# ScalarE writes v's rounded part from PSUM and VectorE takes v's remainder there, in a two-layer attention and coupling kernel

## The reference

```
x = x + attention(layernorm(x))
x = x + coupling_network(layernorm(x))
```

```
k = apply_rope(x @ Wk.T)
v = x @ Wv.T
q = apply_rope(einsum('btd,hkd->bhtk', x, Wq))
w = softmax(where(causal, q k^T * HS**-0.5, -inf))
out = (w v, heads side by side) @ Wo.T
```

## The kernel before, in words

| bank of | is next taken by | VectorE's steps just ahead of its `project` step |
|---|---|---|
| project (group 0, tile 0) | project (group 0, tile 2) | turn_p (1, 1), norm of group 1, scores (2, 3) |
| project (group 0, tile 3) | turn_p (2, 2) | scores (3, 0), scale of group 1, close 1 |
| project (group 1, tile 0) | turn_p (3, 2) | norm of the next batch's group 0, close 2 |
| project (group 1, tile 1) | turn_p (3, 3) | turn_p (3, 1), turn_p (3, 2) |

## Time and profile before

### The profile page before, as it was taken

The page is one execution under the profiler, slowest core; times in us unless marked ns, Lnnn a source line. Parts: engine busy times, 40 slices in busy tenths (PEclk is TensorE's granted clock), DMA queues, the critical chain, the costliest instruction groups (busy, mean ns, idle before and its releaser), DMA issues. The chain is left out here.

```text
span 926.4 us, 15342 instructions
## 1 busy us (share of the span) xinstructions
PE 814.3 (88%) x4368; PEld 644.3 (70%) x4368; DVE 720.2 (78%) x1567; ACT 464.4 (50%) x1020; POOL 363.7 (39%) x377
## 2 busy tenths in 40 slices
PE   4689999998999989999999789988879889999952
PEld 3578788887888868888888557666656666666731
DVE  6779898896998978989978736777777878776575
ACT  2355565554565645565555255444444445444421
POOL 4535644364256434642460014333333334333331
PEclk9889999999999999999999899877897989877865
DMA  6000011101110110011000250000000100000011
GB/s 186 1 1 29 19 46 47 46 1 50 46 36 12 47 49 24 24 47 46 2 0 2 81 192 1 23 24 23 19 28 0 41 27 24 24 24 23 11 35 45
DMA packets 34588, 32.60 MB, mean 35 GB/s; under 512 B 3524, under 2 KB 34244, under 8 KB 34500
## 3 DMA queue, kind: packets, MB, share of 16 engines
q1 hardware_dynamic: 34500, 31.56, 10.7%
HBM read 16.88 MB, written 14.68 MB: 34 GB/s over the span
## 5 line engine op out<-in xcount | busy, mean ns | idle before, releaser
L507 ACT ACTIVATE pT_hi<-bank 128x512 fp32r<-128x512 f32 x192 | 90.9, 492 | 104.6 <-PE bank L843 96.1
L554 ACT ACTIVATE x_all<-scores_ps,neg_max 128x384 f32<-128x384 f32 (+7 forms) x128 | 94.6, 739 | 46.3 <-DVE neg_max L684 42.4
L580 DVE TENSOR_TENSOR pT_lo<-bank,pT_hi 128x512 fp32r<-128x512 f32 x192 | 100.7, 547 | 21.3 <-ACT pT_hi L507 21.3
L684 DVE TENSOR_REDUCE neg_max<-scores_ps 128x1 f32<-128x384 f32 (+7 forms) x128 | 95.3, 749 | 23.9 <-PE scores_ps L816 17.9
L843 PE MATMUL bank<-ident,x_all 128*128 128x128 f32 x576 | 92.7, 279 | 22.3 <-DVE pT_lo L580 17.3
L384 POOL TENSOR_TENSOR rope_a<-x_all,cos_sb 128x384 f32<-128x384 f32 x60 | 61.7, 1028 | 116.7 <-ACT x_all L507 112.6
L1342 PE MATMUL cycle_ps<-h,w_sb 128*128 128x512 f32 x192 | 92.3, 617 | 12.0 <-ACT h L1108 12.0
L843 PEld LDWEIGHTS bank<-ident,x_all 128*128 128x128 f32 x576 | 66.6, 142 | 35.4 <-DVE pT_lo L580 22.3
L1057 POOL TENSOR_TENSOR h_w<-h,w_sb 128x256 f32<-128x256 f32 x48 | 35.6, 742 | 113.1 <-ACT h L1122 113.1
L731 PE MATMUL oT_ps<-pT_hi,v_hi 128*128 128x512 f32 x192 | 77.3, 402 | 0.5 <-DVE oT_lo L580 0.4
L731 PE MATMUL scores_ps<-k_hi,q_hi 128*128 128x512 f32 (+1 forms) x192 | 71.6, 373 | 0.0
(11 more groups left out here) (132 smaller groups left out, 2120.3 us busy)
## 6 DMA issues: line engine op xcount, KB each, us to landing
x_all<-x SPq DMA_DIRECT2D x16, 512.0 KB, 3.6
out<-x_all SPq DMA_DIRECT2D x16, 512.0 KB, 3.0
x<-x_all SPq DMA_DIRECT2D x12, 512.0 KB, 3.0
x_all<-x SPq DMA_DIRECT2D x6, 1024.0 KB, 5.9
x_all<-wqkv SPq DMA_DIRECT2D x1, 512.0 KB, 4.6
sin_sb<-sin_t SPq DMA_DIRECT2D x1, 512.0 KB, 7.0
cos_sb<-cos_t SPq DMA_DIRECT2D x1, 256.0 KB, 5.8
x_all<-wo SPq DMA_DIRECT2D x1, 256.0 KB, 5.9
```

The lines of the kernel that those rows point to most:

```text
L507: return nc.scalar.activation(out, in_, ACT.Copy)
L554: nc.scalar.activation(probs[u % 2][:, k, 0:keys], scores_ps[k % 2][:, 0:keys], ACT.Exp, bias=neg_max[:, u * G + k:u * G + k + 1], accum_o ...
L580: return dve.tensor_tensor(out, whole, hi.bitcast(F32), ALU.subtract)
L684: dve.tensor_reduce(neg_max[:, u * G + k:u * G + k + 1], scores_ps[k % 2][:, 0:keys], AX_X, ALU.max, negate=True).then_inc(max_ready, 1)
```

## The change

ScalarE no longer copies the whole bank. It copies the 384 columns of q and k to qk[t], and with a second instruction the 128 columns of v straight to v_hi. VectorE no longer rounds v. Its `project` step now waits for v_hi and computes v_lo from the PSUM bank. GpSimd no longer waits for v_hi and no longer computes v_lo. Since VectorE is now the last reader of a projected bank, `reader_of` names v_ready, which VectorE's subtraction raises, where it named the semaphore of ScalarE's copy. The step lists of `BATCH_PERIODS` and the order of the banks are unchanged.

```diff
-        qkv = [room(1) for t in range(G)]
+        qk = [room(1)[:, 0:3 * HS] for t in range(G)]
...
-        def split_v(engine, n, i, t):
-            engine.tensor_tensor(v_lo[n][:, i, :], qkv[t][:, 3 * HS:4 * HS],
-                                 v_hi[n][:, i, :].bitcast(F32), ALU.subtract).then_inc(v_ready, 1)
...
                     # gpsimd, project
-                        pool.wait_ge(qkv_ready, tile + 1)
+                        pool.wait_ge(qk_copied, tile + 1)
...
-                        if not first:
-
-                            pool.wait_ge(v_hi_ready, tile + 1)
-                            split_v(pool, n, i, t)
...
                     # scalar, project
                         at_least(act, rot_ready, tile - G + 1)
-                        at_least(act, v_ready, tile - G + 1)
-                        copy(qkv[t][:], ps[:]).then_inc(qkv_ready, 1)
+                        copy(qk[t][:], ps[:, 0:3 * HS]).then_inc(qk_copied, 1)
+
+                        copy(v_hi[n][:, G * g + t, :], ps[:, 3 * HS:]).then_inc(v_hi_ready, 1)
...
                     # vector, project
-                        dve.wait_ge(qkv_ready, bb * TILES + i + 1)
-                        dve.tensor_copy(v_hi[n][:, i, :], qkv[t][:, 3 * HS:]).then_inc(v_hi_ready, 1)
+                        dve.wait_ge(v_hi_ready, bb * TILES + i + 1)
+                        low(v_lo[n][:, i, :], ps[:, 3 * HS:], v_hi[n][:, i, :]).then_inc(v_ready, 1)
...
                             rope_cos(dve, i, t, first_cos_ready)
-                            dve.wait_ge(v_hi_ready, i + 1)
-                            split_v(dve, n, i, t)
...
                 # tensor, reader_of
                 if kind == "project":
-                    return qkv_ready, bb * TILES + G * rest[0] + rest[1] + 1
+                    return v_ready, bb * TILES + G * rest[0] + rest[1] + 1
```

More of the change, by code:

```diff
@@ L353, in attention_phase @@
         projected = sem("projected")
-        qkv_ready = sem("qkv_ready")
+        qk_copied = sem("qk_copied")
         v_hi_ready = sem("v_hi_ready")
@@ L384, in rope_cos @@
             engine.tensor_tensor(rope_a[:].rearrange("p (c d) -> p c d", d=HALF),
-                                 qkv[t][:, 0:3 * HS].rearrange("p (c d) -> p c d", d=HALF),
+                                 qk[t][:].rearrange("p (c d) -> p c d", d=HALF),
                                  cos, ALU.mult).then_inc(ready, 1)
-        def split_v(engine, n, i, t):
-            engine.tensor_tensor(v_lo[n][:, i, :], qkv[t][:, 3 * HS:4 * HS],
-                                 v_hi[n][:, i, :].bitcast(F32), ALU.subtract).then_inc(v_ready, 1)
         @block.sync
@@ L480, in do @@
                             rope_cos(pool, i, t, rope_products)
-                        qk = qkv[t][:, 0:3 * HS].rearrange("p (c e d) -> p c e d", e=2, d=HALF)
+                        halves = qk[t][:].rearrange("p (c e d) -> p c e d", e=2, d=HALF)
                         sin = sin_sb[:, i, :].unsqueeze(1).broadcast_to([P, NH + 1, HS])
@@ L484, in do @@
                             rope_b[:].rearrange("p (c e d) -> p c e d", e=2, d=HALF),
-                            qk[:, :, ::-1, :],
+                            halves[:, :, ::-1, :],
                             sin.rearrange("p c (e d) -> p c e d", e=2),
                             ALU.mult).then_inc(rope_products, 2 if first else 1)
-                        if not first:
-                            pool.wait_ge(v_hi_ready, tile + 1)
-                            split_v(pool, n, i, t)
                         pool.wait_ge(rope_products, (tile + 1) * 2)
```

## The result

The changed kernel takes 980.62 us (median of 4 runs, 972.38 to 982.33), beside 932.37 for the kernel before on the same chip. The ratio is 1.051, with a 95% interval of 1.046 to 1.056. The forecast was 965 with a range of 945 to 976. It had the sign and was too small by 15.6 us. Medians here are over all executions of a kernel, while a ratio leaves out those that lie over 1.5% above the fastest of their kernel.

The account below looks back on a forecast made before the run. TensorE's instruction list was taken to bound the attention. 16.1 (first place) + 13.2 (second place) - 1.9 (gains) + 5.5 (clock) = 32.9 us; with the 926.4 span and 5.8 around it, forecast 965 us, range 945 to 976.

Parts of the forecast that it names:

- The start: TensorE's 7.24 us wait at the start for GpSimd's rot, behind which one 1.11 us subtraction goes: -1.1 us.
- The -0.8 of batch 0: VectorE's scaling in batch 0 waits for rstd behind two GpSimd subtractions that go: 0.8 us gained.
- The two places: Two points in the attention where TensorE waits for a bank until VectorE's `project` step: 16.1 and 13.2 us.
- The first place: `project` of tile 2 reusing tile 0's bank, then a turn needing tile 3's: seven batches 2.3 us late each, 16.1 us.
- second stall: At the first place, TensorE's turn of probabilities waiting for tile 3's bank: forecast 1.95 us.
- The first stall: At the first place, TensorE's `project` of tile 2 waiting for tile 0's bank: 1.31 us, 1.65 in the last batch.
- the second place: Turns (3, 2) and (3, 3) reusing the other group's tile 0 and 1 banks: stalls 2.66 plus 0.3 us, 13.2 in all.
- The rival Half: VectorE makes good the first stall before tile 3, so the first place costs 2.8 us in all: 946 us; 14%.
- Hidden: Rival: the bank wait does not bind because other waits hold TensorE as long: about 932 us; 4%.
- Relief: Rival: VectorE, freed of 17 us, reaches `project` before the bank is wanted, and TensorE's pT_lo waits vanish: 924 us; 5%.
- the clock: TensorE at half clock behind each of four 2.66 us stalls, none behind shorter ones: 1.4 us each, 5.5 in all.
- The rival Clock: Each of 14 stalls lets TensorE's clock fall, 19.2 us for that term: 979 us; 12%.

Follow-up runs that it names:

- experiment 6: Changed kernel with VectorE's `project` steps moved earlier at both places: 935.19 us; at the second place alone: 957.57 us; the latter plus GpSimd waiting for the scalings: 930.91 us.
- Experiment 4: Changed kernel plus one wait: in batches 1 to 7 GpSimd begins rope of tile 1, group 0, only after VectorE's four scalings; 942.76 us, ratio 1.018.
- experiment 1: Kernel before with one word changed: TensorE takes a projected bank only once VectorE has rounded v, not after ScalarE's copy; 966.62 us, ratio 1.038.

## Why the prediction was wrong in size

**The price of the operations: right.** v_lo from PSUM lasts 282 ns on average (273 to 293), as its pT_lo form did. Below it is ScalarE's copy of 384 columns:

```profile
L573 DVE TENSOR_TENSOR v_lo<-bank,v_hi 128x128 fp32r<-128x128 f32 x64 | 17.5, 282 | 5.8 <-ACT v_hi L499 5.8
L499 ACT ACTIVATE x_all<-bank 128x384 f32<-128x384 f32 x64 | 31.3, 489 | 32.5 <-PE bank L724 32.5
```

The 11.2 us on ScalarE stay hidden. With 273 to 293 ns in all 64 cases the subtraction never waits for GpSimd, as the rule of the Trainium skill said that the prediction drew on (SBUF — State Buffer, section "SBUF: two separate sides"), and experiment 6 leaves next to nothing for these operations by themselves.

**The start: right.** TensorE's wait for rot ends at 27.44 instead of 28.39: -0.95 for -1.1. The -0.8 of batch 0 came in part and was lost again: the scaling at 45.02 begins at 43.50, 1.5 us sooner, and takes 4.28 us instead of 3.54, beside four whole instructions of GpSimd.

**The two places: right, and the sum of their waits nearly, by errors that cancel.** Forecast 29.3 us, measured 28.75 as idle time and 32 from start to start, which is how the prediction had worked it out. The first place made a batch 3.3 us late in the one shown and not 2.3 (2.8 to 3.4 in the seven, 22 us in all for 16.1); its second stall is 2.79 to 2.89 of idle time in all of them. The first stall of the last batch makes TensorE 1.3 late and not 1.65. That leaves 10 for all other places, forecast at 13.2. The four turns of the second place come 2.7 us later on average, as the 2.66 had it, but without the 0.3 behind. The waits of 0.65 to 0.72 before turn (0, 2), 4.1 us in six batches, shrank to 0.2, which the prediction had not counted. At the loop's turns the waits for ScalarE's copy went (4.7 us) while shorter ones for v_lo came (1.48 and 1.58). That errors of 6 and 3 us have opposite signs is luck. The rival Half fell: VectorE made nothing good. Hidden and Relief fell with the same rows.

**The failed step.** It is this one: "From there to the `project` step of tile 3 VectorE needs 134.94 - 130.50 = 4.44 us". It took a duration measured before the change for one after it, though the change removes an instruction of GpSimd that stood beside the scalings and shifts the moment at which they begin in GpSimd's list. VectorE needs 147.78 - 142.24 = 5.54 us now. The prediction weighed what GpSimd does to the new subtraction and to the two roundings that go; it did not ask what else on VectorE was paired with GpSimd's instructions, and the trace had them: 3.18 us beside four of GpSimd's, in the middle of the very 4.44 us that were read from the earlier trace rows. These 1.10 us account for the difference between 3.3 us late and 2.3, and for the 6 us that the seven batches came out dearer. Experiment 4 shows that the length of the scalings sets the stall.

**The mis-sized term: the clock, 5.5 forecast and 15 to 18 measured in the attention.** "I expect one behind each of the four long stalls of 2.66 us, and none behind the shorter" failed since the seven second stalls of the first place grew to 2.9 us each and the clock fell behind five of them. This hangs on the failed step: with scalings of 2.9 us (experiment 1) these stalls are 1.8 and left the clock alone. The price of 1.4 us for one drop was nearly right: nine more drops cost 15 us from start to start, 1.7 each, as two of them lasted twice as long as the others. Stalls of 1.07 us left the clock alone, as the prediction had it from its rows. The rival Clock, with 12%, had 19.2 us for this term and 979 in all. It was near in size, though not in its picture of 14 drops: there were ten, against one before. That its 979 is so near to 980.62 is in part luck, as 6 us of the measured span are the coupling phase, which it had at nothing. The Trainium skill's charge of half the slow time (TensorE: Matmul & The Clock Gate, section "HAM oscillation — how this bites in real kernels") is near the trace: (54.6 - 17.1) / 2 = 18.7, beside 18.3 as busy time and 15 from start to start.

**The coupling phase: 0 forecast, 6 measured.** The prediction had "The coupling phase as long as before". Whether a longer attention has to do with it stays open. The matmuls are the same in all kernels run here, and their profiled executions have the phase between 394.6 and 411.7 us, so all of the 6 may be chance.

Sum: 32.9 forecast, less 0.6 on idle time in the attention, plus 12.8 and 6.0 on the clock, plus 1.8 since the start and batch 0 gave back about nothing and not 1.9: 52.9. That is 20.0 us too little in the span. The forecast of the time missed by 15.6 only, since it added 5.8 us around the span where an execution has some 2. Without that the miss would have been some 4 us larger.

## What to carry to other kernels

When the last reader of a buffer moves to another engine, ask at each reuse when that engine, which works in order, comes to the reading step; its own speed hardly matters (282 ns here), what stands ahead of it does (the hold alone cost 3.8%). A duration of VectorE that was measured beside GpSimd can belong to the pair, as that of the scalings does (1.38 alone, 2.9 to 4.3 beside it) and that of v_lo does not: look, at each such row on the path, at what GpSimd runs there before and after the change, and at which moment, also where the change only takes GpSimd's work away. A stall of TensorE of over 2 us should be priced with the clock's fall behind it (here behind 9 of 11 stalls of 2.2 to 3.3 us, while in the kernel before it fell behind a stall of 2.21 and not behind one of 2.51), and a chain that gets longer can carry several stalls over that length at once.

## What the runs showed of the hardware that was not expected

- With a GpSimd instruction of 0.47 us taken away, four VectorE instructions became slower together, from 3.2 to 4.28 us, about 0.4 of it by the missing instruction and 0.7 by the moment at which they begin. With GpSimd idle they take 1.38.
- One more wait on GpSimd made the kernel 38 us faster (980.6 to 942.8), with no work changed.
- About 19 us of added matmuls did not make it slower (980.6 and 966.0), as they filled stalls and kept the clock: 17.1 us at half clock in the attention where it was 54.6.
- The coupling phase, the same instructions in every kernel, took 394.6 to 411.7 us, the longer the longer its clock was low (112.5 to 153.4 us at half clock). The kernel before alone spread from 917.2 to 943.9 us over 55 executions. Even with 10 to 12 executions of a kernel the intervals of the ratios reach 0.3 to 0.5% either way.
